# A fused vision block on one core: the mixer pipeline in four stages, with the order of work written out for every engine

## The reference

```python
# token mixing, each image n
q, k, v = x@Wq+bq, x@Wk+bk, x@Wv+bv            # per head, 4 heads x 64
ew = exp(w_bias * local_mask); ek = exp(k)
y  = sigmoid(q) * (ew @ (ek*v)) / (ew @ ek)
h  = layernorm(y @ out_w + out_b + flatten(x)) * ln_g + ln_b
h  = concat(cls_tok, h)                        # 257 rows
# gated recurrence over the sequence
u  = layernorm(h); r = sigmoid(u@W_r+b_r); i = sigmoid(u@W_i+b_i)
a  = sigmoid(log_a) * r; b = (1-a) * i * (u@W_in+b_in)
s_t = a_t * s_{t-1} + b_t;  h = h + s @ W_out + b_out
# mixture of experts: one shared and 8 routed, top 2, hidden 1024
v  = layernorm(h); gate = top2(softmax(v @ Wr))
h  = h + shared(v) + sum_e gate_e * expert_e(v)
```

## Time and profile before

| | |
|---|---|
| median of 3 runs | 1060.21 us (1058.24 to 1060.82) |
| profiled execution | 1057.7 us |
| its span, first to last instruction | 1055.9 us |
| busy: PE, DVE, ACT, POOL | 959.6, 696.8, 454.5, 376.9 us |
| mean granted TensorE clock | 0.966 |

### The profile page before, as it was taken

One profiled execution on the slowest core, in us unless ns is written; L12 is line 12 of the kernel. 1 busy time (PEld: TensorE's weight loads), 2 busy tenths in 40 slices (PEclk: granted clock), 3 DMA queues, 4 the chain that ended last, 5 costly groups with the idle time before them and its releaser, 6 DMA issues.

```text
span 1055.9 us, 21575 instructions
## 1 busy us (share of the span) xinstructions
PE 959.6 (91%) x6873; PEld 890.7 (84%) x6874; DVE 696.8 (66%) x2095; ACT 454.5 (43%) x1139; POOL 376.9 (36%) x468
## 2 busy tenths in 40 slices
PE   6866888999999999999788999999999999999995
PEld 4645768888888888888788899999999999999995
DVE  4557878888788888788765446465645546564643
ACT  2202324434444444344333355555555555555553
POOL 4334426423334323334312143342352424243222
PEclk9878989999999999999998899999999999999998
DMA  9303211001110001100001373745282734664222
GB/s 272 111 11 95 80 41 48 20 26 40 40 40 30 20 30 40 40 30 24 28 34 58 103 211 49 199 91 154 50 208 46 187 57 98 153 135 117 45 40 31
DMA packets 48165, 82.68 MB, mean 78 GB/s; under 512 B 6417, under 2 KB 30884, under 8 KB 48133
## 3 DMA queue, kind: packets, MB, share of 16 engines
q0 software_dynamic: 31056, 57.46, 22.5%
q1 hardware_dynamic: 17076, 24.84, 8.1%
HBM read 55.32 MB, written 26.96 MB: 78 GB/s over the span
## 4 chain that ended last, share of the span: by engine, by line
PE 43%; issue 28%; DVE 13%; POOL 12%; ACT 1%; POOLq 1%; DMA 0%; DVEq 0%; SPq 0%; ACTq 0%
PE ps_nd L675 15%; PE ps_proj L660 9%; POOL out L621 5%; PE ps_ri L660 4%; PE ps_proj L744 3%; DVE rden L1352 3%; PE ps_ip L660 3%; PE ps_nd L847 3%; PE ps_h L823 2%; POOL h L569 2%; POOL v_rows L506 2%; PE ps_t L751 1%; POOL rstd L502 1%; PE ps_h L834 1%; DVE A L1414 1%
## 5 line engine op out<-in xcount | busy, mean ns | idle before, releaser
L1177 DVE TENSOR_TENSOR GL<-g_act,GH 128x256 fp32r<-128x256 f32 (+1 forms) x424 | 185.3, 439 | 190.8 <-ACT GH L1024 168.7
L675 PE MATMUL ps_nd<-w2h,GH 128*128 128x256 f32 x832 | 248.3, 298 | 25.4 <-DVE GL L1177 12.0
L1019 ACT ACTIVATE g_act<-ps_proj,fcb 128x256 f32<-128x256 f32 (+1 forms) x280 | 130.8, 467 | 309.7 <-PE ps_proj L660 303.5
L675 PE MATMUL ps_nd<-w2l,GH 128*128 128x256 f32 x832 | 235.4, 283 | 0.0
L675 PE MATMUL ps_nd<-w2h,GL 128*128 128x256 f32 x832 | 233.9, 281 | 0.0
L675 PEld LDWEIGHTS ps_nd<-w2h,GH 128*128 128x128 f32 x832 | 157.9, 190 | 35.9 <-DVE GL L1177 12.2
L1024 ACT CAST GH<-g_act 128x256 fp32r<-128x256 f32 x416 | 161.4, 397 | 0.0
L675 PEld LDWEIGHTS ps_nd<-w2l,GH 128*128 128x128 f32 x832 | 158.2, 190 | 0.0
L675 PEld LDWEIGHTS ps_nd<-w2h,GL 128*128 128x128 f32 x832 | 157.7, 190 | 0.0
L660 PE MATMUL ps_proj<-xh,w1h 128*128 128x256 f32 x544 | 116.4, 295 | 9.2 <-issue 4.5
L621 POOL DMA_INDIRECT out<-yb,rows_to x72 | 114.0, 1584 | 16.6 <-issue 12.7
(11 more groups left out here) (272 smaller groups left out, 1874.5 us busy)
## 6 DMA issues: line engine op xcount, KB each, us to landing
R<-v_rows SPq DMA_DIRECT2D x37, 260.0 KB
w1h<-fc_w POOLq DMA_DIRECT2D x9, 1024.0 KB
w2h<-pj_w POOLq DMA_DIRECT2D x9, 1024.0 KB
stage<-fc_w POOLq DMA_DIRECT2D x9, 1024.0 KB
stage<-pj_w POOLq DMA_DIRECT2D x9, 1024.0 KB
v_rows<-tail_rows SPq DMA_DIRECT2D x16, 260.0 KB, 4.1
x<-x SPq DMA_DIRECT2D x16, 256.0 KB, 3.5
out<-yb SPq DMA_DIRECT2D x16, 256.0 KB, 2.1
```

What stands on the lines that cost most here:

```text
L675: last = pe.matmul(banks[a], g[:, j, a * P:(a + 1) * P], w[i][:, j, :], start=(j == 0 and q == 0), stop=(j == HT - 1 and q == 2))
L1019: act.activation(g_act[:, j % G_SLOTS, 0:width], banks[j % len(banks)][:, 0:width], ACT.Gelu_apprx_tanh, bias=fcb[i][:, j:j + 1]).then_inc ...
L1177: dve.tensor_tensor(GL[:, j, 0:width], g_act[:, j % G_SLOTS, 0:width], GH[:, j, 0:width].bitcast(F32), ALU.subtract).then_inc(gl_done, 1)
```

## The change

`DEPTH` goes from 5 to 4: image t-1 goes from its residual to its scan within step t, image t-2 gets `scan_out` and V, image t-3 the routing and the shared expert. There are 19 steps in place of 20. Steps 0 to 3 are an opening, in which the whole of step 3 with the shared expert of image 0 is already there; steps 4 to 15 run in the loop of two; steps 16 to 18 are the drain. `store_base`, `project`'s wait for `gelu_done` and so on move by one image.

The general step is cut into small functions (`turn_y`, `h_out`, `attention`, `hidden(j)`, `ffn_out(j)`, `low(j)`, `gate_a`, ...) and called in a written order, one for each engine. Opening and drain have orders of their own, in which pieces of neighbouring steps are interleaved. PE, ACT, DVE and POOL in the loop:

```diff
+            def step(t, par):                 # PE
+                turn_y; project0; h_out; attention; project1; logits
+                hidden(0); sums0; hidden(1); sums1; hidden(2); hidden(3)
+                turn_u; hidden(4); rank; hidden(5); gates0; turn_v
+                hidden(6); input0; gates1; input1
+                ffn_out(0); ffn_out(1); hidden(7); ffn_out(2) ... ffn_out(7)
+            def step(t, par):                 # ACT
+                copy_yt; exp0; exp1; gelu 0; gelu 1; high 0; gelu 2; gelu 3
+                high 1; copy_u; high 2; gelu 4; tanh0; high 3; high 4; gelu 5
+                share; copy_v; high 5; gelu 6; high 6; tanh1; gelu 7; high 7
+            def step(t, par):                 # DVE
+                ekv0; h_sum; h_norm; ekv1; v_sum; best; u_stats; second
+                u_norm; ratio0; u_low; v_norm; low 0; low 1; ratio1; y_last
+                low 2; places; low 3 ... low 6; slots_out; v_low
+                gate_a; low 7; gate_b; base_sum
+            def step(t, par):                 # POOL
+                rstd_h; affine; rstd_v; rstd_u; out_bias; rows_out
```

In the opening and the drain, what has an image comes in this order on PE from step 3 on, and in the drain:

```diff
+            project1(3); turn_v(image 0); gates0(image 1); turn_y(3); input0(image 1)
+            hidden(3, 0); h_out(3); logits(3); gates1(image 1); sums0(3)
+            hidden(3, 1..4); input1(image 1); sums1(3); hidden(3, 5); turn_u(3); rank(3)
+            hidden(3, 6); gates0(3); attention(3); gates1(3); ffn_out(3, 0..2); input0(3)
+            hidden(3, 7); ffn_out(3, 3); turn_v(3); ffn_out(3, 4); input1(3); ffn_out(3, 5..7)
...
+            turn_y(16); hidden(16, 0); h_out(16); hidden(16, 1); logits(16); hidden(16, 2..3)
+            attention(16); ffn_out(16, 0); hidden(16, 4); ffn_out(16, 1); hidden(16, 5..6)
+            ffn_out(16, 2); hidden(16, 7); rank(16); turn_u(16); ffn_out(16, 3..4); gates0(16)
+            cls_logits; ffn_out(16, 5); turn_v(16); gates1(16); ffn_out(16, 6); input0(16)
+            ffn_out(16, 7); input1(16); logits(17); hidden(17, 0..2); rank(17); ...
+            attention(17); ...; turn_v(17); ...; ffn_out(18, 7)
```

GpSimd's order gets `split_low`'s parts at other places (`low_first`, `low_second` in step 2, `next_low_first`, `next_low_second` in the drain):

```diff
+            rstd_h(2, 0)
+            affine(2, 0)
+            low_first(1, 1)
+            rstd_u(2, 0)
+            rstd_v(2, 0)
+            low_second(2, 0)
+            out_bias(2, 0)
+            next_weights(2, 0)
...
+            next_low_first(17, 1)
+            rstd_h(16, 0)
```

The class token's routing moves from steps 4 and 5 to step 16 (`CLS_AFTER = NIMG - 2`; `cls_route` on DVE stands there ahead of `gate_a(16)` and `v_low(16)`). Two tiles change places, and the waits with them:

```diff
-        ps_lg = ps_ri[:, 0, 0:2 * LT * NE].rearrange("p (t e) -> p t e", e=2 * NE)
+        ps_lg = ps_h[:, 0, 0:2 * LT * NE].rearrange("p (t e) -> p t e", e=2 * NE)
...
-                        last = pe.matmul(ps_h[:, lt, :], HS[:, k, lt * P:(lt + 1) * P],
+                        last = pe.matmul(ps_ip[:, lt, :], HS[:, k, lt * P:(lt + 1) * P],
...
             def y_out(n):
-                after(pe, h1_done, n - 1)
+                after(pe, hx_done, n)
+                if live(n - 3):
+                    pe.wait_ge(run_ready, n - 2 + past_cls(n - 3, 1))
...
             def input_gate(n, e):
                 if e == 0:
                     after(pe, b_done, FT * n)
+                    after(pe, h1_done, n)
...
             def logits(t, par):
+                    pe.wait_ge(vl_done, n + 1)
+                    pe.wait_ge(hx_done, at_most(n + 3, NIMG))
...
             def hidden(t, par, j):
+                    if j == 0:
+                        pe.wait_ge(vl_done, n + 1)
+                        after(pe, gelu_done, HT * n)
+                        pe.wait_ge(ekv_done, at_most(LT * (t + 1), LT * NIMG))
```

More of the change, by code:

```diff
@@ L283, in vit_tower @@
         cls_row1, cls_s = sem("cls_row1"), sem("cls_s")
-        DEPTH = 5
+        DEPTH = 4
         PEEL = DEPTH + DEPTH % 2
[L292 to L302, removed]
+        PEEL = 4
         def live(n):
@@ L610, in experts_pool @@
+            out_bias(18, 0)
+            rows_out(18, 0)
         def experts_pool(pool):
@@ new lines, in mixer_tensor @@
+            turn_v(3, 1)
+            ffn_out(3, 1, 4)
+            input1(3, 1)
+            ffn_out(3, 1, 5)
+            ffn_out(3, 1, 6)
+            ffn_out(3, 1, 7)
+            with pe.Fori(PEEL // 2, NIMG // 2) as pair:
+                step(pair * 2, 0)
+                step(pair * 2 + 1, 1)
+            project0(16, 0)
+            turn_y(16, 0)
+            project1(16, 0)
+            hidden(16, 0, 0)
+            h_out(16, 0)
+            hidden(16, 0, 1)
+            logits(16, 0)
@@ new lines, in mixer_vector @@
+            gate_a(1, 1)
+            h_norm(2, 0)
+            ekv1(2, 0)
+            gate_b(1, 1)
+            ratio0(2, 0)
+            u_stats(2, 0)
+            ratio1(2, 0)
+            v_sum(2, 0)
+            u_norm(2, 0)
+            ekv0(3, 1)
+            y_last(2, 0)
+            u_low(2, 0)
+            v_norm(2, 0)
+            v_low(2, 0)
+            ekv1(3, 1)
+            h_sum(3, 1)
+            best(3, 1)
+            h_norm(3, 1)
+            low(3, 1, 0)
+            gate_a(2, 0)
@@ new lines, in mixer_vector @@
+            places(3, 1)
+            slots_out(3, 1)
+            gate_b(3, 1)
+            base_sum(3, 1)
+            cls_v(2, 0)
+            with dve.Fori(PEEL // 2, NIMG // 2) as pair:
+                step(pair * 2, 0)
+                step(pair * 2 + 1, 1)
+            ekv0(16, 0)
+            ratio0(16, 0)
+            h_sum(16, 0)
+            low(16, 0, 0)
+            best(16, 0)
+            second(16, 0)
+            ratio1(16, 0)
+            h_norm(16, 0)
+            low(16, 0, 1)
@@ new lines, in mixer_vector @@
+            y_last(16, 0)
+            v_sum(16, 0)
+            ekv1(16, 0)
+            low(16, 0, 2)
+            u_stats(16, 0)
+            ratio0(17, 1)
+            low(16, 0, 3)
+            ratio1(17, 1)
+            low(16, 0, 4)
+            low(16, 0, 5)
+            u_norm(16, 0)
+            u_low(16, 0)
+            v_norm(16, 0)
+            places(16, 0)
+            low(16, 0, 6)
+            slots_out(16, 0)
+            h_sum(17, 1)
+            low(16, 0, 7)
+            h_norm(17, 1)
@@ new lines, in mixer_vector @@
+            y_last(17, 1)
+            cls_route(16, 0)
+            ratio0(18, 0)
+            gate_a(16, 0)
+            v_low(16, 0)
+            best(17, 1)
+            u_stats(17, 1)
+            second(17, 1)
+            ekv0(17, 1)
+            gate_b(16, 0)
+            u_norm(17, 1)
+            places(17, 1)
+            low(17, 1, 0)
+            base_sum(16, 0)
+            low(17, 1, 1)
+            v_sum(17, 1)
+            low(17, 1, 2)
+            slots_out(17, 1)
+            gate_a(17, 1)
```

1159 lines of the change are left out of this document (782 added, 377 removed).

## The result

The changed kernel takes 1014.53 us (median of 4 runs, 1012.52 to 1017.15) against 1059.22 us before: ratio 0.9578, 95% interval 0.9556 to 0.9599. Forecast were 1018 us, 998 to 1042. The profiled execution's span is 1012.9 us, 43.0 less.

What follows compares the result with a forecast made beforehand. PE was taken as the bound, VectorE close behind. Step 4's start 107 + 4 + loop 373.2 + drain 61 = 545.2 against 588.6; less 1.5 for hand-over, 42 us gained: 1018 us, range 998 to 1042.

Steps and rivals of the forecast that it cites:

- Opening: Steps 0 to 3, bound by one image's chain: V of image 0 at 72 us, step 4 starts at 107 (98 to 116).
- Step 4's surcharge: First loop step: rstd_h(4) waiting behind GpSimd's scatters, and the late scan, cost some 4 us.
- Loop: Steps 4 to 15: twelve steps at 31.1 us (29.9 to 33.0), 373.2 us in all.
- The walk: Written order followed through one loop step: PE waits at hidden(0), turn_u 0.2, gates0 0.3; step ends at 30.0 us.
- restarts and small gaps: Loop step's additions: restart after a wait 0.3 to 0.4 three times; 1.2 us of small gaps within the 31.1.
- VectorE within 3 us of PE: Loop: VectorE's work nearly as long as PE's step, the scan having 2.9 us of slack.
- `places` off GpSimd's path: Loop: places runs while GpSimd is idle, so VectorE gets back about 1.1 us a step.
- Drain: Steps 16 to 18: 49.5 us dense, stalls and 2 for the clock, 61 us (50 to 71), 28.6 less.
- Hand-over: Mixer's end to routed experts: last slots ready 3 us ahead of the last piece, not 9; adds 1.5 us (0 to 5).
- (c): Rival, chance 0.08: loop from slots_out through scatters and rstd_h back loses 5 us a step; slower than before, 1077 us.
- (b): Rival, chance 0.10: written orders tighter than the walk; step 30.2, opening 100, drain 56; 995 us.
- (a): Rival, chance 0.19: only the ends gain; loop stays at 31.9 or slows to 32.5, opening costs 5 more; 1040 us.

Runs made afterwards that it cites:

- f1: On top of e1, GpSimd's low_first and low_second moved right behind out_bias(1) in the opening: 1003.97 us, ratio 0.9477.
- e4: The changed kernel with the loop's order of work in the opening too, low_first also moved ahead of cls_rstd: 1020.53 us, ratio 0.9631.
- e1: The changed kernel with one swap in PE's loop step, project1 ahead of attention: 996.23 us, ratio 0.9400.
- e2: The changed kernel with GpSimd's out_bias one wait later in the loop, so that it falls on VectorE's work: 1015.3 us, ratio 0.9594.
- f2: On top of e1, the drain's split of the second expert's weights done on VectorE in four parts instead of GpSimd: 997.42 us, ratio 0.9419.
- f3: On top of e1, the class token's routing on VectorE in the drain cut in two, second part behind v_low(16): 998.84 us, ratio 0.9431.
- g1: On top of e1, both drain edits, f2's split on VectorE and f3's routing in two parts: 995.23 us, ratio 0.9391.

## Why the prediction was right

The time was 3.5 us under the forecast, and the likeliest case came. 2.5 of the 3.5 us are a correction in the sum that did not come: the profiled execution was 2.5 us under the median of the runs before, and equal to it after (1014.52 and 1014.53). The rest are errors of both signs that mostly cancel, which is luck. Step by step:

| term | forecast | measured |
|---|---|---|
| step 4 starts at | 107 (98 to 116) | 106.47 |
| step 4 over a mean step | +4 | +1.5 |
| a loop step, step 4's surcharge apart | 31.1 (29.9 to 33.0) | 30.81 (30.93 with it) |
| drain to the first `CXH` piece | 61 (50 to 71) | 65.4 |
| last piece to R's transpose, over before | +1.5 | +2.7 (11.8 against 9.1) |
| routed experts | 450 | 449.9 |
| last piece | 545.2 | 543.1 |

**Opening.** The size was right, and so were its parts: V of image 0 was forecast on PE at 72 us and stands there at 71.17, and from there to step 4 it is 35.3 us for 35. `low_second` does fall on VectorE (3.68 us for `v_norm`). I called it a point against the order; f1 shows that behind `out_bias(1)` the splits cost more, as the class token's chain is hit. The own order, with its place for the split, is worth 6 us (e4).

**Step 4's surcharge** was too big by 2.5 us. PE's only wait in step 4 is the one for E, 1.3 us in place of 0.7, and the clock falls behind it; no wait for the scan or for what follows `rstd_h(4)` reaches PE.

**Loop.** The number was near, for reasons that only half held. The walk had `hidden(0)` wait for the second `ekv`; it does, for 0.7 us a step, and it is PE's only wait. The walk's other waits (`turn_u` 0.2, `gates0` 0.3) do not show. Its 30.0 us is what the short steps take (29.98). e1's steps without any wait take 29.26, so the dense step is 29.3 and not 28.7, and the wait of 0.68 costs its length and no restart of 0.3 to 0.4 in a short step. What the walk lacked is the clock, which makes seven of twelve steps 1.5 us longer. I wrote that a steadily busy PE had the full clock in the loop. With the clock the wait costs 1.56 us a step on average, over twice its length. That was in the sum by luck, under the names of restarts and small gaps. The price of the wait was the biggest thing to be had in this kernel (18.3 us), and I had read past it: the piece that could be pulled ahead (`project1`) stood in my own walk, directly behind `attention`.

**VectorE within 3 us of PE.** Not the bound. e2 gave it 1.1 us a step more without any effect, and e1 shortened the step by 1.6. The slack of the scan was 4 us in the trace after (it ends at 293.5 us, `attention` starts at 297.4).

**`places` off GpSimd's path.** Right as a duration: `v<-rtanh` takes 0.17 us where one took 1.29. Worth nothing as time in this loop, to go by e2, where the same amount of VectorE's time more did not show. What the Trainium skill (SBUF — State Buffer, section "SBUF: two separate sides") says of the shared port pair, that it is an exclusive lock held for a whole instruction, agrees with the four collisions above (0.69 to 5.40, 0.42 to 1.52, 1.39 to 6.20, 0.17 to 2.29 us). That who starts first holds it, as I wrote in the prediction, does not show in the records' start times: the add's began 0.16 us ahead of GpSimd's, and it was the add that stood still.

**Drain.** The term that was too small, by 4.4 us. The drain of the change as a stretch:

```profile
477.65:543.09 65.44, 57.40 (x419) 55.12 (x418) 51.78 (x184) 23.55 (x61) 30.08 (x28) 0.92 0.12 44
```

PE idles for 8.0 us of it, less than the 10 us of stalls that I had added up. It is busy for 57.4 us, where I had 49.5 of dense work and 2 for the clock: what was mis-sized is the busy time. At a mean clock of 0.92, the clock alone is worth some 5 us (estimate, 0.08 of 65.4). Of the stalls I named, PE waits 3.2 us for VectorE's `run` behind the class token's routing (forecast 3), and 1.5 for the low part of a gelu (1). Missing was `next_low_first`: I had it on GpSimd without looking for what VectorE does in its 4.7 us. In the change it costs PE 1.8 us (a wait shown without a releaser, at the logits behind `base_sum`'s add), 3.0 in e1. Yet taking it away (f2), cutting the class token's chain (f3) and both (g1) changed PE's idle time in the drain only by -0.6, +1.0 and -0.9 us: the drain is a chain of short links, and a wait taken from one comes back at the next. I had priced the stalls one by one as if each were worth its length.

**Hand-over.** +2.7 for +1.5, and PE waits 2.54 us for R. The reason was right: the last scatter began 5.3 us ahead of the last piece before (583.32 in the earlier trace rows) and 2.5 us behind it after. That is a shift of 7.8 us, and I had 6.

**The rivals.** (c), the closed loop of scatters and `rstd_h`, needed 5 us of loss a step; none is to be seen. (b) is what e1 turned out to be, 996 us for its 995, from other parts: it had the step at 30.2, the opening at 100 and the drain at 56, and e1 has 29.4, 106.1 and 67.6. (a) asked for a loop no faster than before; it was 11 us faster.

## What to carry over

When a loop leaves the bound engine a single short wait, look first for work in the same step that doesn't need the thing waited for, and pull it ahead; such a wait can cost twice its length, if the clock falls behind it. Take a stall's worth from an experiment and not from its length: in the loop it was worth more, and in the drain most of it was waited for again at the next link. When two runs differ by no more than a few us, compare their loops and clocks too before the edit gets the credit. Before placing a long GpSimd operation on SBUF, list what VectorE does in its span, the 0.15 us operations on the critical chain above all.

## What was not expected of the hardware

A wait of 0.68 us in a loop where PE is otherwise busy for over 97% was followed by a granted clock of 0.50 (1.2 GHz) in steps 4 and 5 and then in every second step, and by 1.00 in the others. The kernel before had two gaps of 0.6 to 0.7 us a step at another place, and f2 waited for 0.54 us at `project1`; both loops showed 1.00 throughout.

In e1's drain VectorE's record began ahead of GpSimd's by 0.16 us (459.47 and 459.63), and the add stood still all the same, through both of GpSimd's operations (4.67 us and then its own 0.7). The 128x2 operations of f1 began while one of GpSimd's operations ran and came through when that one had ended: one passed per operation of GpSimd (2.29 us, then the next 2.25), and none waited for two.
